# GpSimd subtracts a head's six key tiles in one instruction, and a head's probabilities lie together

## The reference

```python
x = x + tanh(g_xattn) * attention(layernorm(x), ctx)   # 8 heads of 64; keys and values from both
x = x + tanh(g_ffn) * moe(layernorm(x))                # 8 experts, the best 2 by gate, and a shared one

sim  = einsum('bihd,bjhd->bhij', q, k) * 64 ** -0.5     # 256 queries x 768 keys for each batch and head
attn = softmax(sim, axis=-1)
out  = einsum('bhij,bjhd->bihd', attn, v)               # then @ Wo + bo
```

## Time and profile before

| what | value |
|---|---|
| median of 3 runs | 173.44 us (171.92, 173.44, 175.43) |
| profiled execution | 172.02 us, span of its instructions 169.7 us |
| mean granted TensorE clock | 0.988 of full |
| TensorE busy | 139.7 us (82%), 1,724 matmuls |
| VectorE busy | 131.2 us (77%) |
| GpSimd busy | 126.8 us (75%) |
| ScalarE busy | 109.6 us (65%) |

### The profile page before, as it was taken

How to read it: one execution, slowest core, us unless ns; L and a number is a source line. 1 busy time by engine, 2 the same in 40 slices (tenths; PEclk the granted TensorE clock), 3 DMA queues, 4 the chain that set the end, 5 groups by cost and what they waited for, 6 DMA issues and landing times.

```text
span 169.7 us, 4332 instructions
## 1 busy us (share of the span) xinstructions
PE 139.7 (82%) x1724; PEld 111.5 (66%) x1724; DVE 131.2 (77%) x255; ACT 109.6 (65%) x182; POOL 126.8 (75%) x90
## 2 busy tenths in 40 slices
PE   7789588558699989999998892979866995999953
PEld 4435234335478768787787792869856994999952
DVE  1779999667667868768869689989999889454691
ACT  3369583329969979899968998569523462555600
POOL 7609999919999999989777955596557585868750
PEclk9999999999999999999999999999996999999999
DMA  4598699990004800995000000340000000100000
GB/s 136 184 315 211 196 238 242 220 251 14 6 0 85 198 1 16 217 233 191 4 4 0 4 0 0 108 144 6 2 0 0 4 0 4 31 0 4 0 0 31
DMA packets 12925, 13.99 MB, mean 82 GB/s; under 512 B 1470, under 2 KB 9579, under 8 KB 12907
## 3 DMA queue, kind: packets, MB, share of 16 engines
q1 hardware_dynamic: 12906, 13.73, 30.4%
HBM read 7.18 MB, written 0.26 MB: 44 GB/s over the span
## 4 chain that ended last, share of the span: by engine, by line
PE 32%; DVE 28%; POOL 10%; ACT 9%; DMA 8%; SPq 6%; issue 5%; DVEq 0%; ACTq 0%
PE banks L906 5%; DVE kab L852 5%; PE banks L908 5%; PE banks L907 5%; POOL kab L549 4%; ACT kab L642 4%; DVE v_lo L720 3%; DMA kab<-k_nat 3%; DVE nmax L735 3%; PE banks L1006 3%; PE banks L1007 3%; PE banks L987 3%; DMA ring<-in_L_ffn_w_dram 3%; SPq L425 2%; DVE gtop L763 2%
## 5 line engine op out<-in xcount | busy, mean ns | idle before, releaser
L549 POOL TENSOR_TENSOR kab<-kab 128x1024 f16<-128x1024 f32 (+1 forms) x18 | 41.1, 2283 | 17.3 <-DVE kab L852 17.3
L521 POOL TENSOR_TENSOR p_lo<-prob,p_hi 128x768 f16<-128x768 f32 x31 | 50.3, 1642 | 3.1 <-ACT p_hi L606 2.6
L642 ACT ACTIVATE kab<-banks,b1T 128x256 f32<-128x256 f32 x72 | 28.2, 478 | 24.3 <-PE banks L908 15.9
L735 DVE TENSOR_REDUCE nmax<-banks 128x1 f32<-128x768 f32 x32 | 30.5, 954 | 12.5 <-PE banks L988 12.5
L598 ACT ACTIVATE prob<-banks 128x768 f32<-128x768 f32 x32 | 25.8, 805 | 9.1 <-PE banks L1007 8.1
L906 PE MATMUL banks<-wf,kab 128*128 128x128 f16 x144 | 26.2, 224 | 5.8 <-POOL kab L549 4.5
L606 ACT ACTIVATE p_hi<-prob 128x768 f16<-128x768 f32 x32 | 27.0, 843 | 1.0
L852 DVE CAST kab<-kab 128x1024 f16<-128x1024 f32 (+1 forms) x19 | 19.5, 1031 | 9.8 <-ACT kab L642 9.8
L908 PE MATMUL banks<-wf,kab 128*128 128x128 f16 x144 | 26.2, 224 | 0.0
L907 PE MATMUL banks<-wf,kab 128*128 128x128 f16 x144 | 26.2, 224 | 0.0
L1006 PE MATMUL banks<-qab,kab 128*128 128x256 f16 x96 | 23.0, 273 | 0.7 <-DVE qab L832 0.7
(11 more groups left out here) (144 smaller groups left out, 340.3 us busy)
## 6 DMA issues: line engine op xcount, KB each, us to landing
ring<-in_L_ffn_w_dram SPq DMA_DIRECT2D x16, 256.0 KB, 4.1
kab<-k_nat SPq DMA_DIRECT2D x4, 384.0 KB, 4.4
kab<-k_nat SPq DMA_DIRECT2D x6, 192.0 KB, 4.4
kab<-k_nat SPq DMA_DIRECT2D x2, 576.0 KB, 7.2
qab<-qo SPq DMA_DIRECT2D x2, 384.0 KB, 6.2
kab<-k_nat SPq DMA_DIRECT2D x2, 288.0 KB, 7.8
prob<-in_ctx_dram SPq DMA_DIRECT2D x2, 256.0 KB, 5.4
ring<-in_L_xattn_Wk_dram SPq DMA_DIRECT2D x2, 256.0 KB, 3.9
```

Source lines behind the costliest of these rows:

```text
L521: nc.gpsimd.tensor_tensor(p_lo[:, j % 3, dst, :], prob(j, g)[:, 0:n, :], p_hi[:, j % 3, dst, :], ALU.subtract).then_inc(pl_done, 1)
L549: nc.gpsimd.tensor_tensor(hid_lo[:, k % HB, cols], hid[:, k % 2, cols], hid_hi[:, k % HB, cols], ALU.subtract).then_inc(hl_done, 1)
L642: nc.scalar.activation(hid[:, k % 2, c * T1:(c + 1) * T1], span(2 * (k % 2), HC * T1)[:, c * T1:(c + 1) * T1], ACT.Gelu, bias=b1T[:, e * H ...
L735: nc.vector.tensor_reduce(nmax[:, i, q:q + 1], span(0, KEYS), AX_X, ALU.max, negate=True).then_inc(max_done, 1)
```

## The change

A head's six tiles of `prob` lie together in the buffer, where before all first halves stood ahead of all second halves. GpSimd subtracts 6 x 256 = 1,536 elements a partition in one instruction for heads 0 to 14, which waits until ScalarE has written both halves of p_hi. For head 15 it does the first half, as before, and VectorE the second. pl_done counts one for each head. So the exponentials of both halves wait for the whole subtraction of head j-2, and TensorE waits for the whole head ahead of the first key tile of values; the wait ahead of the fourth is gone (that for VectorE's half of head 15 stays).

```diff
--- before.py
+++ after.py
@@ -143,12 +143,12 @@
 
 def lo_tiles(j):
 
-    return 3 if j < LO_LAST else 0
-
-
-def pool_lo(j, g):
-
-    return 2 * j + g + 1 - max(0, j - LO_LAST + (g == 1)) if j >= 0 else 0
+    return KT if j < LO_LAST else KT // 2
+
+
+def pool_lo(j):
+
+    return j + 1 if j >= 0 else 0
 
 
 HB = 3
@@ -207,12 +207,11 @@
         prob_all = sb("prob", [P, 2 * 2 * 3 * T1], F32)
         ctx_sb = prob_all[:, 0:B * T2 // P * D].rearrange("p (t d) -> p t d", d=D)
 
-        prob_one = prob_all[:, 0:2 * 3 * T1].rearrange("p (a t n) -> p a t n", a=2, t=3)
-        prob_two = prob_all[:, 2 * 3 * T1:].rearrange("p (a t n) -> p a t n", a=2, t=3)
+        prob_two = prob_all[:, :].rearrange("p (a t n) -> p a t n", a=2, t=KT)
 
         def prob(j, g):
 
-            return (prob_one, prob_two)[g][:, j % 2]
+            return prob_two[:, j % 2, 3 * g:3 * g + 3]
 
         xT = sb("xT", [P, 2, B * T1], F16)
         cT = sb("cT", [P, 2, B * T2], F16)
@@ -514,11 +513,10 @@
             for t in range(NT):
                 nc.gpsimd.tensor_tensor(x_sb[:, t, :], x_sb[:, t, :], bo_sb[:, :], ALU.add).then_inc(xb_done, 1)
 
-            def prob_lo(j, g):
-                pool.wait_ge(ph_act, 2 * j + g + 1)
-                n = lo_tiles(j) if g else 3
-                dst = slice(3 * g, 3 * g + n)
-                nc.gpsimd.tensor_tensor(p_lo[:, j % 3, dst, :], prob(j, g)[:, 0:n, :], p_hi[:, j % 3, dst, :],
+            def prob_lo(j):
+                n = lo_tiles(j)
+                pool.wait_ge(ph_act, 2 * j + 2 * n // KT)
+                nc.gpsimd.tensor_tensor(p_lo[:, j % 3, 0:n, :], prob_two[:, j % 2, 0:n, :], p_hi[:, j % 3, 0:n, :],
                                         ALU.subtract).then_inc(pl_done, 1)
 
             for j in range(1, EARLY):
@@ -528,9 +526,7 @@
 
             for i in range(STEPS):
                 if 0 <= i - HI_LAG < NH:
-                    prob_lo(i - HI_LAG, 0)
-                    if lo_tiles(i - HI_LAG) > 0:
-                        prob_lo(i - HI_LAG, 1)
+                    prob_lo(i - HI_LAG)
                 for b, s in tail_of(i - 1):
                     if s == TAIL_WO:
                         t = NT + QT * b
@@ -594,7 +590,7 @@
             def exp_half(j, g):
                 act.wait_ge(score_ps, 2 * j + g + 1)
                 if j >= 2:
-                    act.wait_ge(pl_done, pool_lo(j - 2, g))
+                    act.wait_ge(pl_done, pool_lo(j - 2))
                 nc.scalar.activation(prob(j, g), span(2 + 2 * g, 3 * T1).rearrange("p (t n) -> p t n", t=3), ACT.Exp,
                                      scale=DH ** -0.5 / S_SCORE).then_inc(exp_done, 1)
 
@@ -837,8 +833,7 @@
             def last_lo(j):
 
                 dve.wait_ge(ph_act, 2 * j + 2)
-                n = lo_tiles(j)
-                nc.vector.tensor_tensor(p_lo[:, j % 3, 3 + n:6, :], prob(j, 1)[:, n:, :], p_hi[:, j % 3, 3 + n:6, :],
+                nc.vector.tensor_tensor(p_lo[:, j % 3, 3:6, :], prob(j, 1), p_hi[:, j % 3, 3:6, :],
                                         ALU.subtract).then_inc(pd_done, 1)
 
             for i in range(STEPS):
@@ -1027,13 +1022,12 @@
 
                 b, h = divmod(j, HEADS)
                 if q == 0:
-                    pe.wait_ge(pl_done, pool_lo(j, 0))
+                    pe.wait_ge(pl_done, pool_lo(j))
                     if j >= 1:
                         pe.wait_ge(o_done, j)
                 cols = slice(q * P, (q + 1) * P)
                 for t in range(KT):
                     if q == 0 and t == KT // 2:
-                        pe.wait_ge(pl_done, pool_lo(j, 1))
                         if j == LO_LAST:
                             pe.wait_ge(pd_done, 1)
                     vh, vl = v_hi[:, b * KT + t, h, :], v_lo[:, b * KT + t, h, :]
```

## The result

The changed kernel took 175.24 us (median of 4 runs, 173.36 to 176.54) against 172.68 for the kernel before beside it; the ratio is 1.0164, with a 95% interval of 1.0101 to 1.0226. The forecast was 174.8 us, in the range 172.2 to 177.2, with 0.85 for a change within 2%. So it is slower, as forecast, by about 2.8 us where 1.4 was forecast. Timed again in 12 runs it came to 1.0102 (1.0034 to 1.0169); the two intervals overlap, and together they say 1% to 1.7%. (A ratio leaves out, on both sides, the runs that took over 1.5% longer than the fastest of the same kernel, which keeps 3 of those 12, so it is not the ratio of the medians: that is 1.0148 at first and 1.0164 in the repeat.) The profiled execution took 174.62 us, its span is 172.4.

A forecast was written before the change was run, and what follows sets the result against it. TensorE's pace, not GpSimd, was taken to bound the attention stage. Terms 0.16 + 0 + 1.1 + 0.1 gave about +1.4 us, so 174.8 us on the median of 173.44, range 172.2 to 177.2.

The forecast's parts named there:

- Price of one instruction: GpSimd's subtraction of 1,536 elements takes 3,106 ns against 3,284 for two; 2.7 us less busy time over 15 heads.
- The start: TensorE's values(0) waits for head 0's whole subtraction and ends at 47.49 instead of 47.33: +0.16 us.
- The steady heads: GpSimd hands over each head later, but the wait is absorbed: 0, up to +0.2 us.
- rival three: The hand-over loop between GpSimd and TensorE becomes the bound, slower: 176.5 us, or 177.9 with a 3.5 us instruction; chance 0.13.
- The exponentials' wait: Exponentials wait for the buffer until the whole subtraction two heads back is done: 0 us.
- VectorE behind GpSimd: Long subtractions of heads 12 and 13 hold VectorE's L679 and batch 0's normalisations, delaying exp(15,0): +1.1 us, bounds 0 and +1.6.
- The first rival: Both normalisations of batch 0 run ahead of head 13's subtraction, leaving only the start's +0.2: 173.6 us; chance 0.20.
- After the attention: The untouched feed-forward stage moves as a block, with +0.1 us for phases that fall less well.
- The scatter: The kernel's runs lie within 1% of their median, 171.92 to 175.43; about 2%, 3.5 us, can be told from no change.

The follow-up runs named there:

- zeros: Changed kernel with 16 matmuls of zeros on TensorE ahead of values(0): ratio 1.0107; with 8 and three waits on GpSimd: 0.9973.
- head 12 split: Changed kernel with head 12 alone subtracted in two instructions, one profile: exp(13,1) to exp(15,0) took 6.65 us; its run time was not compared.
- head 0 split: Changed kernel with head 0 alone subtracted in two instructions: ratio 1.0101 to the kernel before.
- behind xn: Changed kernel with GpSimd waiting for batch 0's two normalised row tiles ahead of head 13's subtraction: ratio 0.9977 to the kernel before.

## Why the prediction was right

The direction, the range and the decisive mechanism hold. That 174.8 came so close to 175.24 is in part luck: the kernel before, on whose median of 173.44 the forecast stands, had 172.68 beside the changed one, 0.76 lower, and the medians lie 2.56 us apart where 1.4 was forecast. Taken by its steps:

- **Price of one instruction**, 3,106 ns forecast from a line through two rows: 3.10 us. Right to 0.01 us, and so is the statement that the saving has no taker.
- **The start, +0.16.** Right where the clock stayed: 5.07, 5.08 and 5.01 against 4.87 is +0.14 to +0.21. In the profiled execution it was +1.57, since values(0) and the scores after it ran at a granted clock of 0.50 until about 49.3. The sum had no term for the clock, and what it cost there, 1.4 us, outweighs the hold in the profiled one (its lucky 0.62 us at lo(0) hid part of it). It is a matter of the execution: over all profiles the start had the lower clock in 5 of 7 with head 0 whole and no zeros, in 2 of 5 with head 0 in halves, and in neither with zeros. That the longer wait makes it likelier is argued from these counts, not shown; splitting head 0 didn't move the ratio (1.0101 against 1.0102), though it did the medians (1.0057 against 1.0164).
- **The steady heads, 0 to +0.2.** +0.15; the pitch is 3.40, GpSimd waits 0.29 us a head for hi(j,1). The loop that was rival three did not close, since the instruction stayed at 3.10.
- **The exponentials' wait, 0.** Right: exp(2,0) came 3.18 us behind lo(0) in place of 1.73, so it moved by 1.45 where 1.46 was worked out, and in the trace no later one waited for GpSimd.
- **VectorE behind GpSimd, +1.1.** The mechanism and the place are shown, by taking the cause away in three ways (two short instructions, the order turned round, each head by itself), and the size is 1.20. L679 is held for 0.49 us, forecast at 0.5 or more; with that both normalisations come behind the start of head 13's subtraction, as forecast, and the pair takes 3.25, forecast at over 3; exp(15,0) is 6.85 behind exp(13,1), forecast 6.75. That L679 would lose 0.46 us was an estimate from the copy at L807 (768 ns in place of 170); it lost 0.32 (0.49 in place of 0.17). In the traces of the changed kernel the scalar operations were held to the end of the GpSimd instruction (L675 took 0.49 for 0.17 and ended at 91.40 against 91.37; L682 took 2.99 for 0.33 and ended at 96.14 against 96.06), and the statistics of L670 inside the same subtraction were not (0.49 for two). With head 12 split the normalisation that came 0.13 us ahead of the subtraction went first. No semaphore of the kernel accounts for the holds: L675 follows VectorE's own instructions, and rstd, for which L682 waits, was written at 91.48 + 0.73 = 92.21. So GpSimd held VectorE up here beyond what their semaphores ask. What tells the operations that are held from those that aren't, no run shows.
- **The first rival** (the normalisations slip in) had its condition met in the profile with head 12 split and still did not happen: a lead of 0.13 us let one of them through, and the second, which follows it by 0.26 us, came behind GpSimd's. "The second is behind lo(13)" stood among the arguments against this rival, and it was the right one.
- **After the attention, +0.1.** A and B are +0.23 and +0.22, 0.45 together, so this term was too small by 0.35. A varies that much between profiles; B doesn't (43.56 and 43.57 in the two without the change), and its 0.2 has no cause found.
- **The scatter.** The prediction says that the runs lie within 1% of their median; 175.43 is 1.15% above 173.44. Nothing rests on the difference.

## What to carry to other kernels

Joining two instructions on an engine with slack saved nothing here and nearly doubled the time for which it held the neighbour's normalisation (2.99 us for one of them in place of 1.68, where 0.33 is usual). Before fusing, look for short instructions of the neighbour whose duration in the trace is many times their usual one and whose end falls on an end of that engine: here 2.36 us against 0.67 for two was to be seen in the trace before, and it told where the loss would be and about how large. If the long instruction is wanted, put it behind the short ones by a wait; here 0.86 us more of idle time on GpSimd ahead of head 13 (1.61 in place of 0.75) cost less than the hold (5.89 against 6.85), while the waits added in both stages to the kernel before brought 0.7 us in all.

## What the runs showed of the hardware that was not expected

The granted clock of TensorE fell to half after idle times of 0.88 and 1.08 us with nine matmuls between them (head 0 split; the kernel before kept 1.00 with 0.93 and 1.08), and did not fall after 2.92 us without any (behind xn), in kernels whose work up to there is nearly the same. The cost is 0.8 to 1.4 us each time (start 5.89 to 6.50 against 5.0 to 5.1 with head 0 whole, 6.14 against 4.88 with halves). These counts are of 14 profiles in all. A profile of one execution can't say whether an edit brought it on; a stretch's granted clock has to be read in each of several before time is put down to it.
